# Half-size row transposes in the Householder steps of a spectral graph network, with TensorE's program of the steps written out

## What is computed

```python
# layer 0
h = relu(layernorm(x))
x = x + conv(relu(conv(relu(conv(h, W1)), W2)), W3)     # conv(x, W): (adj * adj) @ (x @ W)
# layer 1
h = relu(layernorm(x))
deg = adj.sum(0) + adj.sum(1) - diagonal(adj)
L_norm = d_inv_sqrt[:, None] * (diag(deg) - adj) * d_inv_sqrt[None, :]
_, U = eigh(L_norm)
agg = einsum('mn,bnd->bmd', U.T, h)
x = x + einsum('nm,bmd->bnd', U, relu(agg @ V1 + b1) @ V2 + b2)
```

## Time and profile before

| what | value |
|---|---|
| median of 3 runs | 2256.89 us |
| the profiled execution | 2256.79 us |
| its span, first to last instruction | 2255.1 us |
| TensorE matmuls busy | 2230.2 us, 99% |
| TensorE weight loads busy | 1910.3 us, 85% |
| VectorE busy | 1905.2 us, 84% |
| ScalarE, GpSimd busy | 1153.6 and 1160.4 us, 51% each |
| granted TensorE clock | 1.00 of full speed |

### The profile page before, as it was taken

How to read it: one execution, slowest core, us unless ns; L and a number is a source line. 1 busy time by engine, 2 the same in 40 slices (tenths; PEclk the granted TensorE clock), 3 DMA queues, 4 the chain that set the end, 5 groups by cost and what they waited for, 6 DMA issues and landing times.

```text
span 2255.1 us, 47515 instructions
## 1 busy us (share of the span) xinstructions
PE 2230.2 (99%) x12586; PEld 1910.3 (85%) x12586; DVE 1905.2 (84%) x10565; ACT 1153.6 (51%) x2901; POOL 1160.4 (51%) x1889
## 2 busy tenths in 40 slices
PE   8999999999999999999999999999999999999999
PEld 6788888888888888888888888888888888889998
DVE  7999999888888888888777778989999997557776
ACT  5555555555555555555555554444444444345554
POOL 6555555554555555555555557544555554343332
PEclk9999999999999999999999999999999999999999
DMA  3000000000000000000000000000000001024443
GB/s 106 29 29 29 29 11 29 29 29 29 20 29 29 29 29 28 19 19 28 28 28 28 29 29 20 29 29 20 29 27 22 27 28 38 19 81 133 135 131 107
DMA packets 90030, 90.13 MB, mean 40 GB/s; under 512 B 5376, under 2 KB 89088, under 8 KB 89856
## 3 DMA queue, kind: packets, MB, share of 16 engines
q1 hardware_dynamic: 89856, 88.23, 12.4%
HBM read 54.66 MB, written 33.55 MB: 39 GB/s over the span
## 4 chain that ended last, share of the span: by engine, by line
PE 96%; DVE 2%; POOL 1%; ACT 1%; issue 0%; DVEq 0%; ACTq 0%; POOLq 0%
PE ps L1549 79%; PE ps L1739 10%; PE ps L1471 4%; PE ps L1749 1%; PE ps L1682 1%; DVE A L962 0%; PE ps L1568 0%; POOL w3sum L546 0%; DVE prods L999 0%; PE ps L1636 0%; PE ps L1638 0%; PE ps L1637 0%; PE ps L1639 0%; PE ps L1628 0%; ACT squares L710 0%
## 5 line engine op out<-in xcount | busy, mean ns | idle before, releaser
L502 POOL COPY Eb<-sc 128x1 f32<-128x1 f32 (+1 forms) x254 | 46.7, 184 | 434.8 <-DVE v L1051 220.0
L1549 PE MATMUL ps<-agg2T,w 128*128 128x256 f32 x1024 | 239.2, 379 | 0.0
L1549 PE MATMUL ps<-hid2T,xin 128*128 128x256 f32 x1024 | 236.1, 379 | 0.7 <-ACT h2T L755 0.7
L1549 PE MATMUL ps<-weightT,hid 128*128 128x256 f32 x1024 | 236.7, 379 | 0.0
L1549 PE MATMUL ps<-w,aggT 128*128 128x512 f32 x512 | 231.7, 592 | 0.0
L1549 PEld LDWEIGHTS ps<-weightT,hid 128*128 128x128 f32 x1024 | 189.5, 191 | 36.7 <-issue 14.3
L1549 PEld LDWEIGHTS ps<-hid2T,xin 128*128 128x128 f32 x1024 | 189.0, 190 | 26.2 <-ACT h2T L755 1.1
L1549 PEld LDWEIGHTS ps<-agg2T,w 128*128 128x128 f32 x1024 | 188.5, 190 | 25.5
L755 ACT ACTIVATE hid2T<-ps 128x512 f32<-128x512 f32 x256 | 151.1, 590 | 100.1 <-PE ps L1549 99.0
L1165 DVE SCALAR_TENSOR_TENSOR ahead<-ps,ne,ahead 128x14 f32<-128x14 f32 (+1 forms) x1020 | 189.6, 227 | 0.0
L1162 DVE RECIPROCAL ps<-ahead 128x14 f32<-128x14 f32 (+1 forms) x1024 | 187.9, 229 | 0.1
(11 more groups left out here) (387 smaller groups left out, 6166.1 us busy)
## 6 DMA issues: line engine op xcount, KB each, us to landing
xl<-in_x_dram SPq DMA_DIRECT2D x64, 256.0 KB, 2.8
xr<-in_x_dram SPq DMA_DIRECT2D x64, 256.0 KB, 2.9
x_dram<-xr SPq DMA_DIRECT2D x64, 256.0 KB, 2.3
xin<-x_dram SPq DMA_DIRECT2D x64, 256.0 KB, 2.8
out_dram<-xin SPq DMA_DIRECT2D x64, 256.0 KB, 2.3
w<-in_L_gnn_W_dram SPq DMA_DIRECT2D x1, 2048.0 KB, 10.5
w<-in_L_gnn_W_dram SPq DMA_DIRECT2D x1, 1024.0 KB, 12.4
w<-in_L_gnn_W_dram SPq DMA_DIRECT2D x1, 512.0 KB, 5.7
```

The lines of the kernel that those rows point to most:

```text
L502: pool.tensor_copy(Eb[:, bass.ds(k, 1)], sc[:, 4:5])
L1549: ins = pe.matmul(dst, a, b, start=start, stop=stop, skip_group_check=plan_.units[i][0][0] in "PG")
```

## The change

`row` gets the first live row. Where that lies in the second half of a block (64 or more rows in), the transpose reads partitions 64 to 127 of the column alone, broadcast to 128 columns, against the lower right quarter of the identity, and writes only columns 64 to 127 of that block's row. The steps pass k + 1 as that first row, so k has to be a number when the program is made: the loop over pairs 12 to 20 on TensorE is replaced by written-out pairs. The loops of the other engines stay, and so do the order and the matmuls of the pairs. `p_turn[k % 2]` and `blocks(k)` are what the old arguments gave as well.

```diff
-            def row(dst, col, bl):
+            def row(dst, col, bl, first=0):
 
                 for b in bl:
-                    ins = pe.transpose(dst[:, P * b:P * b + P], col(b).to_broadcast([P, P]), ident[:, 0, 0:P])
+                    c = P // 2 if first - P * b >= P // 2 else 0
+                    ins = pe.transpose(dst[:, P * b + c:P * b + P], col(b)[c:P, :].to_broadcast([P - c, P]),
+                                       ident[c:P, 0, c:P])
                 return ins
...
-            def step_x(k, bl, bank):
+            def step_x(k):
                 pe.wait_ge(col_ready, k + 1)
-                row(bank, lambda b: col[:, b:b + 1], bl).then_inc(xrow, 1)
-
-            def step_q(k, bl):
+                row(p_turn[k % 2], lambda b: col[:, b:b + 1], blocks(k), k + 1).then_inc(xrow, 1)
+
+            def step_q(k):
                 pe.wait_ge(q_ready, k + 1)
-                row(p_q, lambda b: qcol[:, b:b + 1], bl).then_inc(qrow, 1)
+                row(p_q, lambda b: qcol[:, b:b + 1], blocks(k), k + 1).then_inc(qrow, 1)
...
-            def pe_steps(t, first_step, k0, steps, work_beside):
-                for s in range(steps):
-                    step_x(first_step + s, blocks(k0 + s), p_turn[(k0 + s) % 2])
-                    for i, m in work_beside[s][0]:
-                        work(t, i, m, m + 1)
-                    step_q(first_step + s, blocks(k0 + s))
-                    for i, m in work_beside[s][1]:
-                        work(t, i, m, m + 1)
-
             for (first, last, steps, share), k0 in zip(GROUPS, FIRST_STEP):
                 work_beside = beside(steps, share)
-                if last - first == 1:
-                    pe_steps(first, k0, k0, steps, work_beside)
-                else:
-                    with pe.Fori(first, last) as t:
-                        pe_steps(t, steps * t + (k0 - steps * first), k0, steps, work_beside)
+                for t in range(first, last):
+                    for s in range(steps):
+                        k = k0 + steps * (t - first) + s
+                        step_x(k)
+                        for i, m in work_beside[s][0]:
+                            work(t, i, m, m + 1)
+                        step_q(k)
+                        for i, m in work_beside[s][1]:
+                            work(t, i, m, m + 1)
             for k in TAIL:
-                step_x(k, range(NB - 1, NB), p_turn[k % 2])
-                step_q(k, range(NB - 1, NB))
+                step_x(k)
+                step_q(k)
```

## The result

The changed kernel takes 2320.06 us (median, 2319.59 to 2320.78 us) against 2256.78 us for the kernel before beside it: a ratio of 1.0282, with a 95% interval of 1.027 to 1.0294. It is slower by 63.3 us. The profiled execution's span is 2319.0 us, 63.9 us more than before.

The account below looks back on a forecast made before the run. The prediction took TensorE's instruction stream to bound the kernel. It summed -6.6 us for block 0's short transposes and 0 for block 1, VectorE, loop and array changes, from 2256.79 us to 2250.2 us; range 2249 to 2330 us.

Parts of the forecast that it names:

- The bound: Whole kernel: TensorE, busy 99% of the span, sets the time, so a nanosecond off its stream is one off the kernel.
- (1): Steps k = 63 to 126, block 0: 128 short transposes at 0.057 us, not 0.109 us, save 6.6 us.
- (2): Steps k = 191 to 253, block 1: the next matmul pass's load holds 0.11 us, so 126 short transposes save 0.
- rival (B): Short transposes hold the stream as long as whole ones, something other than columns setting 0.109 us: 2256.8 us; chance 0.11.
- (3): VectorE in both windows: it follows, its own chain 0.104 us a step shorter in the first; taken as 0, 0.3 us allowed.
- (5): Short transposes in both windows: 508 changes of the array part in use, over 254 visits, taken to cost nothing.
- (4): TensorE's loop over pairs 12 to 20, written out: taken as 0, between -0.9 and +0.9 us.
- Rival (A): At short transposes and what follows: the array drains at each change, making the kernel slower, 2276 to 2359 us; chance 0.43.
- light form: Drain rival's lower end: only loads lose their cover, 0.05 or 0.10 us a visit, 19 us in all, 2276 us.
- heavy form: Drain rival's upper end: also the array's tail of 0.164 us at all 508 changes, 83 us more, 2359 us.

## Why the prediction was wrong

The forecast was 2250.2 us; measured were 2320.06 us, with the other sign, inside the range of 2249 to 2330 us. Step by step:

**The bound** was right: TensorE's stream sets the time, and all of the loss stands in it.

**(1) Columns.** The price of 64 columns was right: 0.061 us for a second short transpose (0.058 us by single starts) against 0.057 us. By the split above, the saving of 0.052 us is in every visit, under a loss about five times as large.

**(2) The floor by the load** was right. 0.11 us for a matmul's load is what the 64-column matmuls show: 6.5 us saved in place of 27. By this floor block 1's short transposes would have saved nothing even without a drain; no run shows that by itself. The row it was read from, L1595, is one matmul of one column in two passes, not two matmuls. And the 0.07 us each that rival (B) read there is a mean of two unlike distances, 0.028 us to the second pass and 0.112 us behind it: the second is the floor again.

**(3) VectorE** was right in that it sets nothing here. That its own chain would get shorter was wrong, as it hung on (5): its waits for the two rows in the first window went from 26.9 to 57.7 us.

**(4) The written-out loop** was right at 0: ratio 1.0 for it alone.

**(5) The change of rows** is the step that failed. It took nothing for 508 changes, "by the row that is nearest in kind": a matmul pass and a transpose of the same 128 rows alternate without cost. That row says how the array's function can change under way, and nothing of its shape. The runs show 0.094 us at each change, into the 64 rows and out of them, and on top of it the uncovered load behind it. For the term that was put at nothing that makes 508 x 0.094 = 48 us of drains and, by the prices above, about 31 us of loads; less 254 x 0.052 = 13 us for the columns it is 66 us, where 63.3 us were measured. The Trainium skill's rule ("TensorEngine Tiling (Array Packing)", Key Properties: a change of the tiling mode drains TensorE) agrees with these runs, with 0.094 us as the measured size of a drain. Its other half, that a mere change of tile doesn't, no run here shows.

**Rival (A)** was right in mechanism, place and sign. Its two ends were 19 and 102 us, with the measured 63 us between them. They lay so far apart because one term had no price of its own: the light form took the drain at nothing, the heavy form at the array's tail, duration less distance, 0.164 us. The ends in those durations are modelled, and the drain is 0.094 us. With that figure rival (A)'s own formula gives 128 x 0.236 + 126 x 0.290 = 67 us. Its load terms, 0.05 and 0.104 us, were both met to a few nanoseconds. The point from which it decides, 0.026 us a visit, was a tenth of what a visit costs. With so small a saving against 508 changes that no row priced, 0.41 for the forecast rested on little; one outcome can't show what the right chance was. That the measured time lies in the range is due to the room that the range left for (A), not to the forecast.

## What to carry to other kernels

Before an instruction is made shorter by using fewer rows, count the changes of active rows, not the rows saved: with a dense stream of 128-row matmuls around it, each visit to a 64-row form cost 0.23 to 0.29 us here, and to a 32-row form 0.22 us on the average. Only a run of such instructions back to back could earn that: at 0.06 us each in place of 0.11, I estimate that six or seven in a row would break even, which no run here tried. Read the load row beside the matmul row: in this stream a pass was worth shortening down to the load behind it (0.11 us where that is a 32-bit matmul pass's) and no further. And where a saving rests on an operation in a form that the trace doesn't have, a neighbour in form (same rows, other function) is no price for it.

## What the runs showed of the hardware

- A change between 128 active rows and 64 or 32 (partitions 64 to 127 or 96 to 127, in transposes) costs TensorE 0.094 us each way, after passes of 128, 256 and 512 columns alike, and the load behind it starts only with its own matmul (0.046 to 0.05 us for a transpose, 0.104 us for a pass of a 32-bit matmul).
- Matmul row and load row can disagree: short passes are recorded 0.056 us apart, while their loads stand 0.11 us apart, and the next passes make up the difference.
- With 128 rows on both sides weight loads overlap with matmuls in flight: sixteen 128-column passes start 0.111 us apart in the earlier trace rows, while their loads last 192 ns. Behind a change of rows the overlap was lost. The Trainium skill, in "TensorE: Matmul & The Clock Gate", Part 3, on small matmuls packed into one array, has it that weight loads overlap with matmuls in flight only when the row group differs. In this case's stream, which packs none, that condition was not needed.
- Writing nine turns of a TensorE loop out moved 0.34 MB more of instructions and changed the time by less than 0.1%.
